# The last three expert units moved behind the pair columns of a fused convolution and mixture-of-experts kernel, with a shorter gate chain and weighing in products of four tiles

## The reference

```python
agg = jax.ops.segment_sum(msg, dst, num_segments=M).reshape(M, HEADS * NUM_EXPERTS) + b_gat
scores = _layernorm(agg, ln_gamma, ln_beta).reshape(M, HEADS, NUM_EXPERTS).mean(1)
topk_s, topk_i = jax.lax.top_k(scores, TOP_K)
w = jax.nn.softmax(topk_s, axis=-1)
for ei in range(NUM_EXPERTS):
    g = jnp.where(topk_i == ei, w, 0.0).sum(-1)
    hh = jax.nn.gelu(x @ W1[ei] + b1[ei], approximate=False)
    out = out + g[..., None] * (hh @ W2[ei] + b2[ei])
```

## Time and profile before

| | us |
|---|---|
| median of three runs | 768.1 |
| lowest and highest of them | 757.16, 772.35 |
| the profiled execution, on its own clock | 751.74 |
| its span, first to last instruction | 750.0 |
| TensorE busy, share of the span | 555.6 (74%) |
| VectorE busy | 535.5 (71%) |
| GpSimd busy | 419.5 (56%) |
| ScalarE busy | 372.8 (50%) |
| mean granted TensorE clock | 0.87 |
| end of the last pair sum on TensorE | 708.95 |
| start of the weighing on VectorE | 725.67 |

### The profile page before, as it was taken

The page is one execution under the profiler, slowest core; times in us unless marked ns, Lnnn a source line. Parts: engine busy times, 40 slices in busy tenths (PEclk is TensorE's granted clock), DMA queues, the critical chain, the costliest instruction groups (busy, mean ns, idle before and its releaser), DMA issues.

```text
span 750.0 us, 11071 instructions
## 1 busy us (share of the span) xinstructions
PE 555.6 (74%) x3723; PEld 473.9 (63%) x3723; DVE 535.5 (71%) x1609; ACT 372.8 (50%) x1018; POOL 419.5 (56%) x433
## 2 busy tenths in 40 slices
PE   6765765767669798889889889887803676899716
PEld 4655664657558587678778769776603565679615
DVE  6888776686875678877678776685606746678897
ACT  5636554546647567667567657563102222122237
POOL 2063777677777667667778778630771724550022
PEclk9996897788988899999999898998865778999959
DMA  8761665565565576565576565540200631110002
GB/s 265 224 182 51 180 193 171 175 202 161 174 195 153 165 210 183 174 190 171 166 206 174 169 179 158 171 100 8 63 10 4 27 22 24 25 24 1 2 1 112
DMA packets 58197, 94.97 MB, mean 127 GB/s; under 512 B 21916, under 2 KB 36892, under 8 KB 58140
## 3 DMA queue, kind: packets, MB, share of 16 engines
q0 software_dynamic: 25600, 76.50, 35.6%
q1 hardware_dynamic: 32540, 17.75, 9.9%
HBM read 87.49 MB, written 6.71 MB: 126 GB/s over the span
## 4 chain that ended last, share of the span: by engine, by line
PE 32%; POOL 21%; DVE 13%; issue 12%; another core or an unknown queue 9%; ACT 8%; DMA 3%; SPq 0%; DVEq 0%; ACTq 0%; POOLq 0%
POOL arena L484 21%; PE bank L599 7%; PE bank L754 6%; PE bank L666 3%; PE bank L655 3%; ACT arena L882 3%; PE bank L610 3%; PE bank L743 3%; DMA arena<-cells,idx_i 2%; PE bank L579 2%; PE bank L630 1%; ACT arena L967 1%; DVE arena L1286 1%; DVE scratch L1287 1%
## 5 line engine op out<-in xcount | busy, mean ns | idle before, releaser
L484 POOL DMA_INDIRECT arena<-cells,idx_i x288 | 324.1, 1125 | 164.6 <-issue 77.4
L882 ACT ACTIVATE arena<-arena,corner_w 128x128 f32<-128x128 f32 x672 | 206.6, 391 | 60.8 <-DMA arena<-cells,idx_i 54.7
L599 PE MATMUL bank<-ident,arena 128*128 128x128 f32 x1152 | 168.9, 299 | 61.6 <-issue 33.0
L599 PEld LDWEIGHTS bank<-ident,arena 128*128 128x128 f32 x1152 | 146.0, 155 | 96.8 <-issue 67.8
L1111 DVE TENSOR_TENSOR arena<-arena,corner_w 128x640 f32<-128x640 f32 x96 | 79.3, 826 | 68.9 <-DMA arena<-cells,idx_i 62.4
L502 POOL DMA_INDIRECT padded<-src_rows,pk_src x80 | 78.5, 981 | 70.7 <-DVE act_gate L1331 44.1
L896 ACT ACTIVATE scratch<-bank,b_sb 128x512 f32<-128x512 f32 x64 | 43.8, 688 | 131.6 <-remote 66.0
L610 PE MATMUL bank<-dcnw_sb,scratch 128*128 128x128 f32 x576 | 91.6, 298 | 9.3 <-issue 7.2
L890 ACT COPY scratch<-bank 128x384 f32<-128x384 f32 x96 | 45.0, 469 | 104.1 <-remote 80.0
L666 PE MATMUL bank<-w_sb,scratch 128*128 128x128 f32 x512 | 71.2, 298 | 30.2 <-ACT scratch L896 25.3
L610 PEld LDWEIGHTS bank<-dcnw_sb,scratch 128*128 128x128 f32 x576 | 82.1, 213 | 12.7 <-issue 9.1
(11 more groups left out here) (258 smaller groups left out, 633.4 us busy)
## 6 DMA issues: line engine op xcount, KB each, us to landing
arena<-cells,idx_i POOLq DMA_INDIRECT x288
scratch<-in_L_ffn_edge_index_dram SPq DMA_DIRECT2D x32, 128.0 KB
padded<-lo_rows SPq DMA_DIRECT2D x8, 320.0 KB
chan<-in_x_dram SPq DMA_DIRECT2D x4, 512.0 KB, 5.1
cells<-n_tok SPq DMA_DIRECT2D x4, 512.0 KB, 4.2
out_dram<-chan SPq DMA_DIRECT2D x8, 256.0 KB, 2.0
cells<-n_tok SPq DMA_DIRECT2D x4, 448.0 KB, 4.8
padded<-src_rows,pk_src POOLq DMA_INDIRECT x80
```

Of the source, the lines that this page charges most:

```text
L484: nc.gpsimd.indirect_dma_start(cell[:, u, k, :, :].rearrange("p c f -> p (c f)"), None, squares[t // TB], bass.IndirectOffsetOnAxis(ap=idx ...
L599: mm = nc.tensor.matmul(banks[m % 2][:, j * P:(j + 1) * P], cell[:, t % 2, 3 * g + j, c, :], ident[:, :], is_transpose=True, start=(c == 0 ...
L882: ins = nc.scalar.activation(cell[:, u, k, c, :], cell[:, u, k, c, :], ACT.Copy, scale=corner_w[:, t, k, c:c + 1])
```

## The change

The last three units, 29 to 31, leave rounds 4 to 6. Their ups and downs stand on TensorE behind the last pair column, with banks of their own where the reuse of one would make them wait (`UP_BANK`, `DOWN_BANK`), and the Gelu of unit 31 writes to another place (`hid_last`). Their additions on VectorE stand in the gate chain (29 and 30) and in the weighing (31). A Gelu on one element stands before them on ScalarE.

In the gate chain the addition of 1e-16 goes into `own_rows`; the factor 1/std is multiplied in behind the mean over the heads, on 4 values a token instead of 16; each expert's rank comes from one array `beaten_by` of three comparisons an expert, with one reduction; the four gate multiplications are one instruction; the last one itself raises `gates_ready`. VectorE's read of `general_i` stands before the last three columns of round 7.

In the weighing VectorE makes the products of experts 3 and 2 with their gates in place, four tiles in one instruction, and adds the two; the sum is a fourth part for TensorE to turn, and the tokens stay as they are. GpSimd takes expert 1 of three tiles of four instead of two, ScalarE of one instead of two.

```diff
+        TAIL_UNIT = UNITS - 3
+        UP_BANK = {TAIL_UNIT + 1: 2}
+        DOWN_BANK = {TAIL_UNIT + 1: 7, TAIL_UNIT + 2: 2}
...
-                for t in range(4 * g, 4 * g + 2):
+                for t in range(4 * g, 4 * g + 3):
                     ins = nc.gpsimd.tensor_scalar(y_of(t)[:, 1, :], y_of(t)[:, 1, :], gate[:, t, 1:2], None, ALU.mult)
...
-                if n < UNITS:
+                if n < TAIL_UNIT:
                     up(n, 0)
                     up(n, 1)
                 for e in range(NE):
-                    if e == 3 and n < UNITS:
+                    if e == 3 and n < TAIL_UNIT:
                         down(n)
...
+            for n in range(TAIL_UNIT, UNITS):
+                tail_up(n, 0)
+                tail_up(n, 1)
+            for n in range(TAIL_UNIT, UNITS):
+                tail_down(n)
...
-                    parts = [x_tok[:, t, :], y_of(t)[:, 0, :], y_of(t)[:, 1, :]]
+                    parts = [x_tok[:, t, :], y_of(t)[:, 0, :], y_of(t)[:, 1, :], y_of(t)[:, 2, :]]
...
-                    for e in ((0,) if t % 4 < 2 else (0, 1)):
+                    for e in ((0,) if t % 4 < 3 else (0, 1)):
...
+                done(V.tensor_scalar(rows4[:, :, :, 0], rows4[:, :, :, 0], 1e-16, None, ALU.add))
                 done(V.tensor_tensor(big, big, rows4, ALU.add))
...
-                if PAIR_UNIT + p <= UNITS:
+                if PAIR_UNIT + p <= TAIL_UNIT:
                     outputs(PAIR_UNIT + p - 1)
...
+                if p == NSUB - 1:
+                    ve.wait_ge(lost_done, 1)
+                    V.tensor_scalar(general_i[:, :], lost_all[:, :], 0.5, None, ALU.is_gt).then_inc(general_known, 1)
+                    ve.wait_ge(general_known, 1)
+                    general = ve.value_load(general_i[0:1, 0:1], min_val=0, max_val=1)
                 spreads(p, u, 3)
...
-            done(V.tensor_scalar(den, sums4[:, :, :, 0], 1e-16, None, ALU.add))
-            done(V.reciprocal(den, den))
+            done(V.reciprocal(den, sums4[:, :, :, 0]))
...
+            done(V.tensor_tensor(tmp16[:, :, :], tmp16[:, :, :], vec(3), ALU.mult))
+            done(V.tensor_reduce(score[:, :, :], tmp16[:, :, :].rearrange("p i (h e) -> p i e h", e=NE), AX.X, ALU.add))
+            outputs(TAIL_UNIT)
+            outputs(TAIL_UNIT + 1)
             ve.wait_ge(root_done, 2 * B + 1)
             done(V.reciprocal(var, var))
...
+            done(V.tensor_tensor(score[:, :, :], score[:, :, :], var.unsqueeze(2).to_broadcast([P, NT, NE]), ALU.mult))
...
+            products(0)
             for g in range(NT // 4):
...
+                if g + 1 == NT // 4 - 1:
+                    outputs(TAIL_UNIT + 2)
+                    ve.wait_ge(y_ready, UNITS)
+                if g + 1 < NT // 4:
+                    products(g + 1)
+                add_products(g)
```

More of the change, by code:

```diff
@@ L949, in _ @@
                     nc.scalar.activation(dn[:, 0:2, :, :], dn[:, 0:2, :, :], ACT.Exp).then_inc(dn_exp, 1)
+            nc.scalar.activation(warm[:, 0:1], ident[:, 0:1], ACT.Gelu)
+            for n in range(TAIL_UNIT, UNITS):
+                for f in range(NF):
+                    ac.wait_ge(up_done, NF * n + f + 1)
+                    nc.scalar.activation(hid_last[:, f, :] if n == UNITS - 1 else hid[:, (n % 2) * NF + f, :],
+                                         banks[UP_BANK.get(n, 4) + f][:, :], ACT.Gelu,
+                                         bias=b1_sb[:, n % NE, f:f + 1]).then_inc(hid_ready, 1)
             ac.wait_ge(general_known, 1)
@@ L1585, in _ @@
             done(ins)
[L1586 to L1589 removed]
+            done(V.tensor_reduce(beat, beaten_by, AX.X, ALU.add))
             ve.wait_ge(sc_exp, 1)
[L1592 to L1594 removed]
@@ L1595, in _ @@
-            done(ins)
+            done(V.scalar_tensor_tensor(out=gate[:, :, :], in0=beat, scalar=1.5, in1=gate[:, :, :],
+                                        op0=ALU.is_lt, op1=ALU.mult))
             done(V.tensor_reduce(cmp[:, 5, :], gate[:, :, :], AX.X, ALU.add))
             done(V.reciprocal(cmp[:, 5, :], cmp[:, 5, :]))
-            done(V.tensor_tensor(gate[:, :, :], gate[:, :, :], cmp[:, 5, :].unsqueeze(2).to_broadcast([P, NT, NE]), ALU.mult))
-            V.tensor_copy(act_gate[:, 2:3], ident[:, 0:1]).then_inc(gates_ready, 1)
@@ L1602, in _ @@
-            for g in range(NT // 4):
-                for e in (3, 2):
-                    for t in range(4 * g, 4 * g + 4):
-                        ins = V.scalar_tensor_tensor(out=x_tok[:, t, :], in0=y_of(t)[:, e, :], scalar=gate[:, t, e:e + 1],
-                                                     in1=x_tok[:, t, :], op0=ALU.mult, op1=ALU.add)
-                    if e == 3:
-                        done(ins)
-                ins.then_inc(res_ready, 1)
+            V.tensor_tensor(gate[:, :, :], gate[:, :, :], cmp[:, 5, :].unsqueeze(2).to_broadcast([P, NT, NE]), ALU.mult)\
+                .then_inc(gates_ready, 1)
@@ new lines, in four, with products, add_products @@
+            def four(g, e):
+                i = 4 * g % TB
+                return y_img[4 * g // TB][:, i:i + 4, e, :]
+            def products(g):
+                for e in (3, 2):
+                    ins = V.tensor_tensor(four(g, e), four(g, e),
+                                          gate[:, 4 * g:4 * g + 4, e].unsqueeze(2).to_broadcast([P, 4, C]), ALU.mult)
+                st.add(ins)
+            def add_products(g):
+                ve.wait_ge(dve, st.base + st.n - (1 if g + 1 < NT // 4 else 0))
+                V.tensor_tensor(four(g, 2), four(g, 2), four(g, 3), ALU.add).then_inc(res_ready, 1)
```

54 lines of the change are left out of this document (30 added, 24 removed).

## The result

| | median us (runs) | against before, with its 95% interval |
|---|---|---|
| before | 767.4 (20) | |
| changed | 766.1 (20) | 1.0088 [1.0047, 1.0128] |
| changed, once more beside before on one chip (experiment 6; before there 763.7) | 768.9 (12) | 1.0069 [1.0030, 1.0108] |

So the change costs 0.7 to 0.9%, 5 to 7 us. 764.5 us lies near the median, but the forecast was 0.5% less time, and there is more.

The account below looks back on a forecast made before the run. TensorE, with VectorE nearly as full, bounds the pair columns, VectorE's chain the gates, ScalarE the weighing. -2.36 - 2.2 + 1.0 = -3.6 us takes the 768.1 us median to 764.5; range 760 to 771, low end widened to 752.

Parts of the forecast that it names:

- Step 1: Pair columns up to the end of the last pair sum: 2.36 us sooner, bounds 4.4 sooner to 0.3 later.
- The wait of round 5: VectorE's wait for the next column's logits, round 4 to 5: 1.78 us becomes about 0.94.
- the output: VectorE's output addition taken from each of rounds 5, 6 and 7: 0.60 us each, 1.20 for the first two.
- The read in the midst of columns: VectorE's read of `general_i` before the last three columns of round 7: 0.9 us, bounds 0.2 and 1.9.
- step 2: Gates, last pair sum to start of weighing: 3.44 us out, 1.24 added, net 2.2 less, 14.5 us.
- the second output addition: Unit 30's addition in the gates: its down products hidden, with 0.4 us to spare at the full clock.
- the added outputs: Additions of units 29 and 30 moved into the gate chain: 2 x 0.62 = 1.24 us more.
- Step 3: Weighing to the end: last eviction 22.3 us after its start, 1.0 later; bounds 1.4 won, 5.5 lost.
- cold start: TensorE's first weighing transposes at half clock after 7.4 us idle; if warm, last eviction 2.4 us sooner.
- C: Weighing: VectorE's long operations hold GpSimd to 1.3 us each on their shared port; total +0.9 us; chance 0.13.
- A: Pair columns and weighing: TensorE was the bound, both logits waits vanish, transposes warm; -7.5 us; chance 0.17.
- B: Last column round: TensorE's clock falls to half after about 3.4 us idle; total -1.0 us; chance 0.15.

Follow-up runs that it names:

- experiment 6: The unedited changed kernel run once more beside the kernel before on one chip, with round 4 read from traces; 768.9 us, ratio 1.0069.
- gates_only: Kernel before with only the shorter gate chain, units and weighing as before; ratio 0.9956 against before.
- gate_psum: Changed kernel plus one VectorE copy of the gates to PSUM, where its four-tile products read them; ratio 0.9917 against before.
- after2: Changed kernel again with no edit, beside the kernel before on one chip; ratio 1.0069 against before.
- only3: Kernel before with only the changed weighing, units and gate chain as before; ratio 1.0108 against before.
- pool2: Changed kernel with GpSimd at two products a group and ScalarE at six; start of weighing to last eviction 22.93 us.
- undo3: Changed kernel with the weighing of the kernel before put back; ratio 0.9982 against before.
- mix: Changed kernel with its split of work, but VectorE's weighing in short 128-element instructions; start of weighing to last eviction 21.25 us, one run.
- nopool: Changed kernel with no product on GpSimd, VectorE making expert 1's and ScalarE four a group; start of weighing to last eviction 23.28 us, one run.
- psum_warm: Changed kernel with gates read from another PSUM bank and six unread matmuls behind the last expert matmul; ratio 0.9918 against before.
- mix_warm: Changed kernel with VectorE's weighing in short instructions and six unread matmuls before the weighing; ratio 0.9947 against before.
- stay_mix_warm: Short VectorE weighing instructions and shorter gate chain, units left in rounds 4 to 6, 17 unread matmuls; ratio 0.9981 against before.
- the bench: Computation left out: twelve GpSimd products beside one kind of VectorE or ScalarE instruction at a time; 0.58 us a product alone, 1.31 beside 512-element tensor-tensor.

## Why the forecast was wrong

*Step 1, the pair columns: right for rounds 5 and 6, undersized in round 4.* The wait of round 5 went from 1.78 to 0.89 (said: 0.94), that of round 6 from 1.37 to 0.66 (said: 0.54). From l5 to the next logits it is 10.98 us for 12.29, 1.31 less; my working, 0.83 for the wait and 0.60 for the output, gives 1.43. In round 4 the traces without "remote" waits show 1.9 us where I said 0.84 plus 0.60; those waits, 3.0 and 5.1 us in the two executions of the changed kernel, were not in the forecast. The read in the midst of columns took 0.95 us for 0.9. Two slips stand in the working: 0.9 less 0.60 us is 0.3 and not 0.2, and in step 2 half of 1.13 is 0.57 and not 0.54; neither moves the sum by more than 0.1 us.

*Step 2, S to T: right.* 14.1 us for 14.5; no wait before the second output addition; ScalarE's root in time. gates_only shows 3.85 us out for my 3.44, and the added outputs 1.2, as said.

*Step 3, the weighing: this step failed, and with it the sign.* The term was "GpSimd has three instead of two, 0.66 each (median): 2.0 us". That row was measured beside instructions of 128 elements, and the change replaces just these. It measured 1.3 us, so 3.9 a group for as long as VectorE worked, and E came at T + 26.1, not T + 22.3; with the port out of the way (gate_psum) it is 21.6, so the rest of the step (products, transposes, cold start) was sound to 0.7 us. Even VectorE's side was about right (three instructions in 1.95 us for 2.05).

*A term that was not in the sum:* 2.0 us from the last eviction to the end. SyncE waits for TensorE's queue to reach the end of its program, in the changed kernel
```profile
SPq L83 <- PEq L83: 2.1, 1, 2.1
```
where it was 0.2 before. It came out at 2.1 in after2 as well, 1.5 in only3, 0.6 in pool2, 0.2 to 0.3 in undo3, mix, gate_psum, nopool and psum_warm; in mix_warm and stay_mix_warm the stretch from the last eviction is 0.7 us longer than before's. It is not the 16 transposes as such, since gate_psum and mix have them; the changed kernel and only3, which show most of it, are those where GpSimd holds TensorE back early and it then runs its last groups almost without a pause (747.78 to 755.96 above). That is a pattern, not a cause shown; no run tried it.

*Rivals.* C happened: its price of 1.3 us for a GpSimd operation and its mechanism, a turn only between two of VectorE's, are what the runs show, its 0.85 us was passed, and T + 26.8 was said for 26.1. It got 0.13 because 0.66 us beside unbroken short operations seemed to speak against it. It spoke of short ones only: the bench has 0.64 beside that instruction, 0.71 beside a tensor-tensor of the same length, and 1.31 beside one four times as long. C's total of +0.9 us was short by the late end (2.0). From G to the end (-1.7 gates, +4.8, +2.0) and from l5 to G (-2.0) the trace gives 3.0 us more, the comparisons 5.3 and 6.7 with intervals from 2.3 and 3.6; with round 4, 14.9 us in before and 15.3 and 18.2 in the changed kernel, the traces give 3.4 and 6.7. That the "remote" waits make up the rest is not shown: undo3's profiled execution has them too (18.1), and it is no slower than before. A didn't happen (waits stayed; TensorE was idle for 8.0 us and began its transposes at 0.50, 1.2 GHz); B neither, the clock held 1.00 in round 7 and over the 3.1 us of idleness before its first column (3.4 said).

## What to carry to other kernels

Before VectorE's work is merged into fewer, longer instructions, look for what GpSimd does beside them: beside an unbroken row of tensor-tensor instructions of 512 elements from two SBUF tiles, a GpSimd product takes the time of two of them. What VectorE saved here, 2.4 to 1.95 us a group or 3.6 us in all, was paid about twice over on GpSimd, whose 24 products took 22.9 us (8.08 and 14.81) for 24 x 0.66 = 15.8, and which the next stage waits for. A duration read beside one kind of neighbour isn't valid beside another; where a change replaces the neighbour, price the engine that did not change again. If long instructions are wanted, keep one input of the products in PSUM, for which one copy of 0.3 us was enough here.

## What the runs showed that I had not expected

- A tensor-scalar of 512 elements, with one tile in SBUF, slows GpSimd to 0.93 us; at 128 elements it is 0.62.
- scalar-times-plus of 512 slows it to 0.80, tensor-tensor of 512 to 1.31, with two SBUF inputs each.
- TensorE's queue reached its end 2 us late and held the program's end, after the last output had landed (issued at 756.6, 2.0 us to land, end at 761.0).
